# Loops of a routing, expert and scan kernel written out round by round, with constants in their waits

## What is computed

```
x = x + 0.5 * ffn(layernorm(x))     # 8 experts, 2 choices per token, capacity 640 per expert and choice
x = x + attn(layernorm(x))          # mamba block with a scan over time, then a small MLP
x = x + 0.5 * ffn(layernorm(x))     # the same weights as the first

def ffn(h):                         # routing, then the experts
    probs = softmax(h @ gate_w.T + gate_b)
    for c in range(2):              # choice c: expert idx, its place pos within the expert
        keep = pos < 640
        hmid = relu(xb[e] @ W1[e] + b1[e])        # 256 -> 1024
        yb   = hmid @ W2[e] + b2[e]               # 1024 -> 256
        y   += yb[token's slot] * prob * keep

def scan(dt, B, C, u):              # 512 channels x 16 states, over 2048 steps of each sequence
    h = h * exp(dt * A) + (dt * u) * B
    y = sum over states of h * C
```

## Time and profile before

| | us |
|---|---|
| median of 3 runs | 2109.23 |
| lowest and highest run | 2103.46, 2115.71 |
| the profiled execution | 2106.13 |
| its span, from the first to the last instruction | 2104.3 |
| first ffn layer: routing, experts (by the first transposes of the experts) | 0 to 119, 119 to about 530 |
| mamba block; its eight turns | about 530 to 1567; 591.6 to 1519.7 |
| second ffn layer: routing, experts | 1567 to 1678, 1678 to 2104 |

### The profile page before, as it was taken

The page is one execution under the profiler, slowest core; times in us unless marked ns, Lnnn a source line. Parts: engine busy times, 40 slices in busy tenths (PEclk is TensorE's granted clock), DMA queues, the critical chain, the costliest instruction groups (busy, mean ns, idle before and its releaser), DMA issues. The chain is left out here.

```text
span 2104.3 us, 36222 instructions
## 1 busy us (share of the span) xinstructions
PE 1711.2 (81%) x10792; PEld 1417.0 (67%) x10793; DVE 1640.2 (78%) x2887; ACT 985.2 (47%) x1603; POOL 1315.4 (63%) x823
## 2 busy tenths in 40 slices
PE   5379898996578798988898798986757298999996
PEld 5279898996245555655565655655537298999996
DVE  5857676675479999999999999999924776666765
ACT  2333332332266577766767676766521433332331
POOL 1246555457377888878788788888610456454555
PEclk8589999998789799999999999997985599999998
DMA  5244343342345444445444545444306234343341
GB/s 191 90 110 103 73 91 80 76 88 39 140 137 162 144 137 154 140 144 151 140 153 141 143 132 158 143 145 155 105 1 200 81 75 97 72 87 70 83 71 24
DMA packets 161024, 238.02 MB, mean 113 GB/s; under 512 B 29370, under 2 KB 85296, under 8 KB 160304
## 3 DMA queue, kind: packets, MB, share of 16 engines
q1 hardware_dynamic: 130096, 198.84, 30.5%
q0 software_dynamic: 30720, 36.53, 10.4%
HBM read 202.57 MB, written 38.34 MB: 114 GB/s over the span
## 5 line engine op out<-in xcount | busy, mean ns | idle before, releaser
L1367 POOL TENSOR_TENSOR m_dB<-m_DTU,m_BC 128x1024 f32<-128x1024 f32 x256 | 602.8, 2360 | 155.4 <-DVE PS L1460 81.8
L1460 DVE TENSOR_TENSOR_SCAN PS<-PS,m_ST,m_dB 128x512 f32<-128x512 f32 x448 | 553.1, 1272 | 33.8 <-POOL m_dB L1367 26.1
L1155 ACT ACTIVATE PS<-m_DT,m_A 128x512 f32<-128x512 f32 x512 | 332.1, 681 | 212.9 <-DVE m_ST L1476 212.0
L1146 PEld LDWEIGHTS PS<-keep_ident,m_G 128*128 128x128 f32 x2048 | 256.4, 151 | 161.0 <-issue 72.4
L1146 PE MATMUL PS<-keep_ident,m_G 128*128 128x128 f32 x2048 | 296.3, 292 | 61.6 <-POOL m_G L1356 40.7
L1467 DVE TENSOR_TENSOR m_G<-PS,m_BC 128x512 f32<-128x512 f32 x448 | 298.0, 672 | 0.0
L605 PE MATMUL PS<-e_xh,e_wh 128*128 128x256 f32 x1008 | 294.1, 292 | 2.9 <-issue 2.6
L662 ACT ACTIVATE e_hh<-e_u 128x512 fp32r<-128x512 f32 x252 | 157.9, 633 | 283.7 <-DVE e_u L718 275.8
L605 PE MATMUL PS<-e_xl,e_wh 128*128 128x256 f32 x1008 | 288.6, 286 | 0.0
L605 PE MATMUL PS<-e_xh,e_wl 128*128 128x256 f32 x1008 | 288.1, 286 | 0.0
L623 PE MATMUL PS<-e_wh,e_hh 128*128 128x256 f32 x1008 | 281.5, 279 | 0.0
(11 more groups left out here) (205 smaller groups left out, 3098.7 us busy)
## 6 DMA issues: line engine op xcount, KB each, us to landing
m_BC<-bc_rows SPq DMA_DIRECT2D x512, 256.0 KB, 3.8
layer_raw<-w SPq DMA_DIRECT2D x64, 512.0 KB
xrows<-r_xn SPq DMA_DIRECT2D x16, 512.0 KB, 4.2
keep_X<-x SPq DMA_DIRECT2D x4, 1024.0 KB, 9.6
sums<-keep_X SPq DMA_DIRECT2D x4, 1024.0 KB, 11.0
out<-keep_X SPq DMA_DIRECT2D x4, 1024.0 KB, 11.2
keep_X<-sums SPq DMA_DIRECT2D x3, 1024.0 KB, 14.0
e_xin<-xrows,e_gix POOLq DMA_INDIRECT x160
```

The source lines that it names most:

```text
L1146: last = M(PS[:, B_Y + j, ts], G[:, n % NG, j, ts], C["ident"][:, :], is_transpose=True, start=False, stop=(s == DS - 1 and a == CTT - 1))
L1155: return nc.scalar.activation(out, in_, func, **kw)
L1367: G_.tensor_tensor(dB[:, s % 2, :, :], DTU[:, es, :], BC[:, s % NBC, 0:1, :].to_broadcast([P, 2, CT]), ALU.mult).then_inc(dB_ok, 1)
L1460: V.tensor_tensor_scan(HS[:, :] if on_pool(n, j) else state(n, j), state(n, j), dB[:, s % 2, j, :], ST[:, s, e:e + 1], ALU.mult, ALU.add). ...
```

## The change

Every `Fori` of the three stages becomes a Python loop. Its rounds stand one after another in the program of each engine, the counters in the waits and in the slices become constants, and the branches back are gone. The order of the engines' work is the same, and so are buffers, semaphores and DMAs. Eleven loops in the text become the same kind of `for`; those of `chunks` and `run` are one text for several engines:

```diff
-            with dve.Fori(0, HALVES, 1) as h:
+            for h in range(HALVES):
                 statistics(h * 2)
                 statistics(h * 2 + 1)
                 norm(h, 0)
...
-            with gp.Fori(0, QUARTERS, 1) as q:
+            for q in range(QUARTERS):
...
-            with pe.Fori(0, TT // (NH * GT), 1) as i:
+            for i in range(TT // (NH * GT)):
...
         def chunks(eng, step):
 
-            with eng.Fori(0, EXPERTS // 2 - 1, 1) as i:
+            for i in range(EXPERTS // 2 - 1):
                 for c in range(TURN):
                     step(i, c, False)
...
-            with gp.Fori(0, EXPERTS // 2 - 1, 1) as i:
+            for i in range(EXPERTS // 2 - 1):
                 for c in range(BEHIND, TURN + BEHIND):
                     step(i, c)
...
             turn(0, 0, True, False)
-            with eng.Fori(0, MCH // 2 - 1, 1) as i:
-                turn(i * 2 + 1, 1, True, True)
-                turn(i * 2 + 2, 0, True, True)
+            for k in range(1, MCH - 1):
+                turn(k, k % 2, True, True)
             turn(MCH - 1, 1, False, True)
```

More of the change, by code:

```diff
@@ L348, in _ @@
         def _(act):
-            with act.Fori(0, HALVES, 1) as h:
+            for h in range(HALVES):
                 for pair in range(0, NX, 2):
@@ L376, in _ @@
             pe.sem_inc(lg_ok, LG0)
-            with pe.Fori(0, HALVES, 1) as h:
+            for h in range(HALVES):
                 for pair in range(0, NX, 2):
```

5 lines of the change are left out of this document (2 added, 3 removed).

## The result

| | before | after |
|---|---|---|
| median, us | 2108.18 (4 runs) | 2039.62 (4 runs) |
| lowest and highest run | 2103.46, 2115.71 | 2035.39, 2058.32 |
| the profiled execution | 2106.13 | 2038.81 |
| its span | 2104.3 | 2037.1 |

The ratio is 0.9687, with a 95% interval of 0.9654 to 0.972. The direction, the mechanism of the jumps and the two terms of the jumps were right; the odd turns were wrong, the routing's term was too low, and the largest miss, the projection in the routing, had no term at all.

The account below looks back on a forecast made before the run. DVE was taken to bound the scan and PE the expert layers. 7.8 (scan jumps) + 3.3 (odd turns) + 33.3 (experts' jumps) + 3.0 (routing) = 47.4 us less, giving 2062 us; range 2044 to 2078.

Parts of the forecast that it names:

- the mechanism of the jumps: Scan and expert loops: an engine's jump back pauses it, PE's branch 5.7 us in the middle, while leaving the loop doesn't.
- the odd turns: Scan turns 3 and 5: without PE's pause they go as turn 6, DVE's gate waits shrinking, 3.3 us; weak, 0 to 5.
- the routing's term: DVE's loop over halves in routing: register waits vanish, some 0.5 us a quarter, 3.0 us in all; bounds 1 and 6.
- The experts' jumps: Expert layers, PE's four jumps back: 22.3 us of idleness and 11 us at half clock return, 33.3 us; bounds 22 to 33.
- Nothing else is late behind it: Experts, behind PE's jumps: no other engine makes PE wait; DVE's split weights have 0.8 us of slack at the first jump.
- rival (c): Expert steps' matmul pace, 11.75 or 11.34 us, changes: all fast 2046 us, chance 0.09; all slow 2069, chance 0.03.
- (b): Experts: only PE's idleness returns, half-speed stretches stay or DVE becomes late; 31 us gained in all, 2078 us; chance 0.14.
- The scan's jumps: Scan, two jumps back: DVE's idleness of 3.82 and 3.94 us goes whole, 7.8 us, as DVE bounds the scan.
- from then on PE runs without a gap: Second layer's routing: after the first two quarters PE has no gaps, so only those quarters count, 1.0 us.
- (d): All loops: the change does nothing for the time, pauses being unseen code or hidden waits; 2105 to 2109 us; chance 0.04.
- (e): Experts: PE's 34 forward branches over skipped products each cost 5.5 us in code run once; slower, 2249 us; chance 0.04.

Follow-up runs that it names:

- experts_pe: The changed kernel with the experts' loop put back on PE alone, all other engines written out: 2071.70 us, ratio 0.9812 to the kernel before.
- scan_dve: The changed kernel with the scan's loop put back on DVE alone: 2063.95 us, ratio 0.978 to the kernel before.
- scan_loop: The changed kernel with only the scan's loop put back, on all five engines: 2058.71 us, ratio 0.9746 to the kernel before.
- interleave: The changed kernel with PE's routing projection alternating 8 transposes of one group with 16 gate products of the group before: 2055.49 us, ratio 0.9724 to the kernel before.

## Why the prediction was right and where it was wrong

- **The experts' jumps (33.3 us).** Right, and slightly low. The four stretches gave 35.4 us: the steps after the jumps are not only whole again but go at the faster pace, 11.34 to 11.36 us instead of the 11.75 that the sum had put in for them (17.24 or 17.45 instead of 17.85). experts_pe shows that it is PE's jump. The 11 us beside the idleness were not all half clock: by the busy times of the earlier trace rows they are 8.5 us of longer work and 2.6 us of two more waits of PE behind the jumps of the second layer (1.51 us at 1784.0, 1.05 us at 1897.9), which "Nothing else is late behind it" had missed. The other 5.4 us of the stage have two parts. The 2.8 us between the jumps are the unsettled pace, which the prediction had as rival (c): 30 of 53 full steps of the whole stage go at 11.34 to 11.37 us after and 18 of 51 before. Of the 2.6 us in the first ten steps, 0.8 are pace too. The rest is the net of steps before the chunks run full, above all the sixth (7.93 and 7.65 us before, 6.00 and 6.17 after); other traces have it at 6.0 or at 7.6 to 7.7, with and without the loops, so this part of the gain is not the change's. Far from the start the same chunks go fast in every trace with PE written out and narrow gate products, other ones behind a jump of PE, and others again with the wide products. The cause of the pace was not found. "Only the idleness returns" (b) is out, since the clock is 1.00 in all four stretches.
- **The scan's jumps (7.8 us).** Right as a term: scan_dve gives the pause alone, 4.4 and 4.3 us, and scan_loop costs 11.8 us in time.
- **The odd turns (3.3 us).** Wrong. The step that failed is "without the pause turns 3 and 5 go as 6 does". They were compared because they were the turns after a jump, but the wait at the gate alternates by itself. It was 3.28 us in turn 3 after the change, and 3.1 us with PE written out in scan_dve. In the compared pair turns 2, 4 and 6 even took 3.3, 0.6 and 0.7 us more, which ate 4.6 of the 7.8 us. The prediction called the term weak; it should have widened the range by it on both sides.
- **Register arithmetic in the routing (3.0 us).** Right in kind, low in size. A quarter's statistics went from 4.80 us from start to start (1566.05 to 1570.85, the start of the last row) to 4.04, by 0.76 instead of 0.5, since the small operations between the two gaps of the earlier trace rows had their register waits too, each below what a row shows as idleness. With the start of the chain it is 4.1 us.
- **The projection (nothing forecast).** Here is the step that made the forecast miss: "from then on PE runs without a gap", by which the projection was put at nothing. The runs showed 17.1 us there in the compared pair. Averaged over the traces it is about 14.5 us, of which 11 come from the second layer (40.7 us in three traces with the long chain of DVE, 29.6 in ten with the short one and PE written out); the 3.4 of the first layer can't be told from chance. The prediction read the earlier trace rows rightly and took a stage without gaps for one with nothing to gain. It had seen that PE's clock in the first layer is partly full and partly half and may shift, and gave that a bound of 6 us; the second layer's projection, all at half clock, was not looked at as something that could change. A stage that is busy from end to end at 1.2 GHz still had room: 40.7 us became 28.3, and 25.2 with the padding.
- **The rivals (d) and (e).** Neither came. PE's 158 branches over skipped products in after, (ns: shortest, middle, longest):

```profile
L488 PEldq COMPARE_BRANCH  x158: 65/174/537, 131.8 to 2019.7; - x158
```

  None paused in code that runs once, so a forward branch over one chunk's products is cheap whether or not a loop holds the code. The 108 ns of "Advanced Engine Details and Errata" (Control Flow Timing) in the Trainium skill lie among these, and far from the 5.5 us of PE's jumps back.
- **The range.** It left no room for a stage that the sum had no term for. The error of the compared profiled executions, 19.8 us, is made of +19.8 (routing), +7.5 (experts), -7.9 (scan) and +0.5, less 0.1 of rounding. That the scan's miss and the experts' nearly cancel is luck.

## What to carry to other kernels

Count the instructions of a loop's body for each engine, counters and waits included: up to 256 on DVE and ACT and some 1500 on PE a jump back is free in these runs. Beyond, it cost 2.4 to 3.2 us in loops that do nothing else, 3.8 to 4.4 on DVE in the kernel's scan and 5.0 to 7.4 on PE (its branches); why it is more there was not found. It costs this only on the engine that bounds the stage. On PE the restart at a lower clock adds some 40% of the pause (8.5 us to 22.3). When a change moves the start of a stage by a microsecond or two, look at the clock in every stage in which PE does narrow matmuls back to back: here such a stage went at either level, group by group, and padding the products from 8 to 128 columns kept the clock up at no cost.

## What the runs showed of the hardware beside that

- A 128x128 fp32 product with 128 moving columns takes as long as one with 8 (3.84 and 3.74 to 4.06 us for 32 at full clock), and the stage around it is faster, since with the wide ones the clock stays at 2.4 GHz (16 transposes in 1.91 us instead of 3.2 to 3.7).
- PE's clock falls to half without any idleness: in `interleave` after 1.7 us of products and 0.9 us of transposes at full clock, with no gap in the rows.
- DVE's small memsets (28 ns apart) stop for 0.32 us after every 128 instructions in the first round of every loop, and in all rounds of the bodies that pause (the row of 128 memsets ahead of 0.33 us of idleness above); the second and third rounds of the others have no such stop.
- A pause at a jump isn't always over with the first instructions: at 272 memsets DVE did 4 after 3.21 us and stood for another 2.13 us, and at 352 it did 5 after 2.99 us and stood for 2.06. At 384 and more, where the next border is 80 to 90 instructions off, there is no second pause.
